# First sums of an MoE loaded after the fourth scatter, sixteen buffers for the late sums, landed blocks counted by ACT

## What is computed

```python
t = _to_tokens(x1)
xf = _ln_t(t).reshape(N, 128)
probs = softmax(xf @ Wr, axis=0)     # xf: 12544 x 128
vals, idx = top_k(probs.T, 1024)                     # per expert
h = gelu(einsum('ecd,edf->ecf', xf[idx], W1) + b1)   # 128 -> 512
out_e = einsum('ecf,efd->ecd', h, W2) + b2           # 512 -> 128
moe = zeros_like(xf).at[idx].add(vals[..., None] * out_e)
x = from_tokens(t + moe)
```

## Time and profile before

| | us |
|---|---|
| time, median of 3 runs | 484.05 (483.96 to 487.23) |
| span of the profiled execution, first to last instruction | 481.8 |
| last gather of expert 7 landed, in that span | 415.4 |
| the fold's last add | 446.9 |
| the last add of the late stage | 478.7 |
| mean granted clock of PE | 0.838 |

### The profile page before, as it was taken

One profiled execution on the slowest core, in us unless ns is written; L12 is line 12 of the kernel. 1 busy time (PEld: TensorE's weight loads), 2 busy tenths in 40 slices (PEclk: granted clock), 3 DMA queues, 4 the chain that ended last, 5 costly groups with the idle time before them and its releaser, 6 DMA issues.

```text
span 481.8 us, 7878 instructions
## 1 busy us (share of the span) xinstructions
PE 356.9 (74%) x2459; PEld 244.9 (51%) x2459; DVE 314.5 (65%) x1047; ACT 256.3 (53%) x526; POOL 158.5 (33%) x151
## 2 busy tenths in 40 slices
PE   2878998999999978201226769797797797498675
PEld 2435655566555647200113557484673765266564
DVE  3278898799899886788796685657552212229544
ACT  3359898789998873676502446254364344320000
POOL 4000000000000000000047777787888787766000
PEclk9989999899999995555555999898989799789655
DMA  4446577766676653992012232443535199737798
GB/s 108 120 122 185 180 227 250 232 195 223 207 244 228 190 171 106 297 353 87 0 28 55 53 96 54 94 47 84 79 44 87 52 236 316 144 29 163 243 374 323
DMA packets 39121, 76.19 MB, mean 158 GB/s; under 512 B 7056, under 2 KB 19504, under 8 KB 39088
## 3 DMA queue, kind: packets, MB, share of 16 engines
q1 hardware_dynamic: 26976, 60.56, 39.7%
q0 software_dynamic: 9472, 8.72, 11.8%
q10 hardware_dynamic: 2640, 6.51, 3.5%
HBM read 35.03 MB, written 30.39 MB: 136 GB/s over the span
## 4 chain that ended last, share of the span: by engine, by line
PE 37%; ACT 18%; DVE 18%; issue 10%; DMA 8%; POOL 6%; SPq 2%; DVEq 0%; ACTq 0%; POOLq 0%
PE psC L898 8%; PE psC L735 6%; ACT ln_tok L547 5%; PE psB L886 4%; DMA x_pad<-moe_sum_late 4%; PE psB L765 4%; PE psC L886 4%; DVE x_all L1426 3%; POOL moe_sum_late L467 2%; PE psB L753 2%; ACT x_in L607 2%; DVE conv L1054 2%; ACT act L570 2%; ACT signs L607 2%; ACT act L586 2%
## 5 line engine op out<-in xcount | busy, mean ns | idle before, releaser
L438 POOL DMA_INDIRECT picked<-token_rows,slot_idx x32 | 31.4, 981 | 249.2 <-issue 248.9
L735 PE MATMUL psC<-x_pad,tap_diag 64*64 64x392 f32 x384 | 72.8, 528 | 8.0 <-issue 4.3
L735 PE MATMUL psC<-hid,tap_turned 64*64 64x392 f32 x384 | 72.8, 528 | 0.0
L898 PE MATMUL psC<-w,hid 128*128 128x128 f32 x448 | 52.9, 280 | 1.8 <-ACT hid L665 1.7
L898 PEld LDWEIGHTS psC<-w,hid 128*128 128x128 f32 x448 | 52.1, 196 | 4.3 <-ACT hid L665 3.4
L735 PEld LDWEIGHTS psC<-x_pad,tap_diag 64*64 64x64 f32 x384 | 29.8, 142 | 39.4 <-issue 32.0
L886 PE MATMUL psB<-picked_T,w 128*128 128x512 f32 x64 | 38.6, 735 | 5.3 <-ACT picked_T L635 5.0
L665 ACT ACTIVATE hid<-psB,b_T 128x512 f32<-128x512 f32 x32 | 21.8, 686 | 37.3 <-PE psB L886 37.3
L547 ACT ACTIVATE ln_tok<-psA,sm 112x128 f32<-112x128 f32 x112 | 40.9, 477 | 0.9 <-DVE sm L1046 0.9
L467 POOL DMA_INDIRECT moe_sum<-y_rows,slot_idx x24 | 37.7, 1572 | 7.3 <-issue 6.4
L1376 DVE TENSOR_TENSOR y_sum<-psC,b_rows 128x512 f32<-128x512 f32 x14 | 9.7, 691 | 44.3 <-PE psC L898 44.3
(11 more groups left out here) (247 smaller groups left out, 802.1 us busy)
## 6 DMA issues: line engine op xcount, KB each, us to landing
token_rows<-rows SPq DMA_DIRECT2D x16, 422.6 KB, 4.9
x_in<-in_x_dram SPq DMA_DIRECT2D x16, 392.0 KB, 3.3
x_res<-in_x_dram SPq DMA_DIRECT2D x16, 392.0 KB, 4.1
moe_sum<-hid SPq DMA_DIRECT2D x16, 392.0 KB, 4.5
x_all<-x SPq DMA_DIRECT2D x16, 392.0 KB, 3.0
moe_sum_late<-hid SPq DMA_DIRECT2D x16, 392.0 KB, 5.1
out_dram<-act ACTq DMA_DIRECT2D x16, 392.0 KB, 5.8
w<-in_L_ffn_W_dram SPq DMA_DIRECT2D x16, 256.0 KB, 3.4
```

The lines of the kernel that those rows point to most:

```text
L438: nc.gpsimd.indirect_dma_start(out=picked_in[k][:, b, :], out_offset=None, in_=rows_dram, in_offset=bass.IndirectOffsetOnAxis(ap=slot_idx[ ...
L735: ins = nc.tensor.matmul(psC[col * HC:col * HC + HC, half, 0:HALF].rearrange("c (h w) -> c h w", w=W), weights[of, n, :], lines[of, q, dy: ...
L898: ins = nc.tensor.matmul((psA if first else psC)[:, h, b * C:(b + 1) * C], hid[:, f, lo:lo + 128], w2[:, q, f * C:(f + 1) * C], start=(f = ...
```

## The change

The sixteen loads of first sums are issued after the weights of expert 6, once scatters 0 to 3 have landed, and ahead of the weights of expert 7; their other waits go. Their buffers no longer include gather buffers or `x_in`: the four convolution buffers become one tensor `work`, of which seven buffers are cut. The fold stays behind the last expert on PE and DVE (`FOLD_SPOTS`: none, none, all sixteen) and has two PSUM regions. The late sums go into the same sixteen buffers, each as soon as its image's first sums are turned and its blocks landed. ACT counts landed blocks after the last gelu, in place of POOL. The output images lie in `hid`. Stores of images 0 to 7 are issued by SP, each behind a late load from the ninth on; ACT issues those of images 8 to 15. In the last expert DVE does bias and weight of the first half ahead of the norm of the second half's rows. Loops over the late images are written out.

```diff
-FOLDED_EARLY = 0
-BEHIND = 2
+FOLD_SPOTS = (range(0, 0), range(0, 0), range(0, B))
+STORED_BY_SP = 8
...
+        work = sb("work", [128, 8 * HW])
+        conv, act1, act2, x1 = (work[:, 2 * HW * n:2 * HW * (n + 1)].rearrange("c (q n) -> c q n", q=2) for n in range(4))
...
+        turned = TPI * C
+        sums_in = [ln_tok[:, 0, :], ln_tok[:, 1, :], x_pad[0:P, 0, 0:turned], x_pad[0:P, 1, 0:turned]] + [
+            work[0:P, n * turned:(n + 1) * turned] for n in range(7)] + [
+            rows[:, 0, 0:turned], rows[:, 1, 0:turned], logits[:, :], logits_T[:, :],
+            s_cmp[0:P, :, :].rearrange("p b k -> p (b k)")]
+        o_img = [hid[:, k:k + 1, 0:HW] for k in range(ENDS)]
         end_regions = (psB, psD, psA, psC)
-        fold_regions = (psD, psA, psB)
+        fold_regions = (psD, psB)
...
-            for e in range(2, E):
+            for e in range(2, E - 1):
                 sp.wait_ge(s_l2, (e - 1) * 2)
                 load_w(e, e % 2)
             for q in range(2):
                 sp.wait_ge(s_sca[q], 16 * SB * SECOND // 2)
-            sp.wait_ge(s_ge, E - 1)
             sp.wait_ge(s_idx, 2 * E)
             for q in range(2):
                 sp.wait_ge(s_rows[q], 16 * B // 2)
                 sp.wait_ge(s_x1c[q], 16 * B // 2)
             for img in range(B):
-                if img == B // 2:
-                    sp.wait_ge(s_l2, 2 * E - 3)
                 load_first(img)
-            sp.wait_ge(s_fd, 2 * ENDS)
+            sp.wait_ge(s_l2, (E - 2) * 2)
+            load_w(E - 1, (E - 1) % 2)
...
-            for img in range(B):
-                if img >= ENDS:
-                    sp.wait_ge(s_ft, img - ENDS + 1)
+            def load_late(img):
+                sp.wait_ge(s_fd, 2 * img + 2)
                 at = LAST_TILES + img
                 sp.wait_ge(s_landed, sp.value_load(need[at:at + 1, 0:1], min_val=1, max_val=SB))
-                load_y(img, img % ENDS)
+                sp.dma_start(sums_in[img].rearrange("p (t c) -> p t c", c=C),
+                             late_t[:, ds(img, 1), :, :].rearrange("p i t c -> p (i t) c")).then_inc(s_yl[img], 16)
+
+            for img in range(B):
+                load_late(img)
+                if img >= B - STORED_BY_SP:
+                    stored = img - (B - STORED_BY_SP)
+                    sp.wait_ge(s_fa, stored + 1)
+                    sp.dma_start(out_d[:, ds(stored, 1), :], o_img[stored % ENDS]).then_inc(s_fo[stored % ENDS], 16)
...
                         nc.gpsimd.indirect_dma_start(out=sums, out_offset=at, in_=y_rows[:, q, b, :],
                                                      in_offset=None, compute_op=ALU.add).then_inc(s_blk[b], 16)
-                        if b >= BEHIND:
-                            pool.wait_ge(s_blk[b - BEHIND], 16)
-                            pool.sem_inc(s_landed, 1)
...
-            for b in range(SB - BEHIND, SB):
-                pool.wait_ge(s_blk[b], 16)
-                pool.sem_inc(s_landed, 1)
...
-            with act.Fori(0, B // ENDS) as turn:
-                for k in range(ENDS):
-                    act.wait_ge(s_fa, turn * ENDS + k + 1)
-                    act.dma_start(out_d[:, ds(turn * ENDS + k, 1), :], o_img[k]).then_inc(s_fo[k], 16)
+            for b in range(SB):
+                act.wait_ge(s_blk[b], 16)
+                act.sem_inc(s_landed, 1)
+            for img in range(STORED_BY_SP, B):
+                act.wait_ge(s_fa, img + 1)
+                act.dma_start(out_d[:, ds(img, 1), :], o_img[img % ENDS]).then_inc(s_fo[img % ENDS], 16)
...
+            def turn_first(img):
+                region = fold_regions[img % 2]
+                pe.wait_ge(s_yf[img], 16)
+                for a, tiles in enumerate(BANK_TILES):
+                    if img >= 2:
+                        pe.wait_ge(s_fk, img * 2 + a - 3)
...
             def last_expert(e, q, use):
                 pe.wait_ge(s_w1[q], use * 16 + 16)
+                pe.wait_ge(s_idx, E * 2)
+                for img in FOLD_SPOTS[0]:
+                    turn_first(img)
                 turn_picked(e, 0)
                 hidden(e, q, 0, {})
                 pe.wait_ge(s_w2[q], use * 16 + 16)
                 down(e, q, 0)
+                for img in FOLD_SPOTS[1]:
+                    turn_first(img)
                 turn_picked(e, 1)
                 hidden(e, q, 1, {})
                 down(e, q, 1)
+                for img in FOLD_SPOTS[2]:
+                    turn_first(img)
...
+            pe.wait_ge(s_fk, 2 * B)
             pe.wait_ge(s_ptc, E * 2)
-            pe.wait_ge(s_yb, 2 * E - 1)
...
-            pe.wait_ge(s_yr, 2 * E)
             pe.wait_ge(s_yb, 2 * E)
...
+            for img in range(B):
+                pe.wait_ge(s_yl[img], 16)
+                if img >= ENDS:
+                    pe.wait_ge(s_fa, img - (ENDS - 1))
                 for t in range(TPI):
+                    ins = nc.tensor.transpose(end_regions[img % ENDS][:, t // 4, (t % 4) * P:(t % 4 + 1) * P],
+                                              sums_in[img][:, t * C:(t + 1) * C], ident[0:P, 0:P])
                 ins.then_inc(s_ft, 1)
...
             def last_expert(e, q, use):
+                for q_of in range(2):
+                    dve.wait_ge(s_x1c[q_of], 16 * B // 2)
...
                         .then_inc(s_gt, 1)
+                    bias_out(e, h)
+                    weigh(e, q, use, h)
                     if h == 0:
                         norm_picked(e, 1)
-                    bias_out(e, h)
-                    weigh(e, q, use, h)
+                    for img in FOLD_SPOTS[1 + h]:
+                        add_first(img)
...
             dve.wait_ge(s_fk, 2 * B)
+            dve.wait_ge(s_l2, 2 * E)
...
+            for img in range(B):
+                k = img % ENDS
                 dve.wait_ge(s_ft, img + 1)
+                if img >= ENDS:
+                    dve.wait_ge(s_fo[k], img // ENDS * 16)
```

More of the change, by code:

```diff
@@ L166, in build @@
         dist = sb("dist", [128, HW])
-        junk = conv[:, :, :].rearrange("c q n -> c (q n)").bitcast(mybir.dt.bfloat16).rearrange("c (k n) -> c k n", n=HW)
+        junk = work[:, 0:2 * HW].bitcast(mybir.dt.bfloat16).rearrange("c (k n) -> c k n", n=HW)
         exps = sb("exps", [128, HW])
@@ L275, in build @@
         s_ge, s_gt = sem("gate_exp"), sem("gate_ready")
-        s_yl, s_fo = ([sem(f"{name}{k}") for k in range(ENDS)] for name in ("y_loaded", "out_stored"))
+        s_yl = [sem(f"late_y_loaded{k}") for k in range(B)]
+        s_fo = [sem(f"out_stored{k}") for k in range(ENDS)]
         s_ft, s_fa = sem("final_turned"), sem("final_added")
@@ L933, in expert @@
                 down(e, q, 1)
+            def turn_first(img):
[4 more added lines that the diff above has]
+                        pe.wait_ge(s_fk, img * 2 + a - 3)
+                    for t in tiles:
+                        ins = nc.tensor.transpose(region[:, a, (t % 4) * P:(t % 4 + 1) * P],
+                                                  sums_in[img][:, t * C:(t + 1) * C], ident[0:P, 0:P])
+                    ins.then_inc(s_fd, 1)
             def last_expert(e, q, use):
                 pe.wait_ge(s_w1[q], use * 16 + 16)
+                pe.wait_ge(s_idx, E * 2)
+                for img in FOLD_SPOTS[0]:
+                    turn_first(img)
                 turn_picked(e, 0)
@@ L956, in _ @@
             first_expert()
             for e in range(1, E - 1):
-                if e == E - 2 and FOLDED_EARLY:
-                    pe.wait_ge(s_idx, E * 2)
-                    pe.wait_ge(s_ptc, (E - 1) * 2)
-                    for img in range(FOLDED_EARLY):
-                        turn_first(img)
-                    pe.wait_ge(s_fk, 2 * FOLDED_EARLY)
                 expert(e, e % 2, e // 2, e + 3 < E, e + 2 < E)
             last_expert(E - 1, (E - 1) % 2, (E - 1) // 2)
-            pe.wait_ge(s_idx, E * 2)
+            pe.wait_ge(s_fk, 2 * B)
@@ L967, in _ @@
             pe.wait_ge(s_ptc, E * 2)
-            pe.wait_ge(s_yb, 2 * E - 1)
-            for img in range(FOLDED_EARLY, B):
-                turn_first(img)
-            pe.wait_ge(s_fk, 2 * B)
             pe.wait_ge(s_gelu, E * 2 * FT)
-            pe.wait_ge(s_idx, E * 2)
-            pe.wait_ge(s_yr, 2 * E)
             pe.wait_ge(s_yb, 2 * E)
-            def turn_back(img, k, turn):
-                pe.wait_ge(s_yl[k], turn * 16 + 16)
-                if since(img, ENDS):
+            for img in range(B):
+                pe.wait_ge(s_yl[img], 16)
+                if img >= ENDS:
@@ L986, in turn_back @@
                 ins.then_inc(s_ft, 1)
-            for k in range(ENDS):
-                turn_back(k, k, 0)
-            with pe.Fori(1, B // ENDS) as turn:
-                for k in range(ENDS):
-                    turn_back(turn * ENDS + k, k, turn)
         @block.vector
@@ L1425, in add_first @@
                     kept = x1_all[:, img * HW + lo:img * HW + lo + n]
```

(16 more changed lines are left out.)

44 lines of the change are left out of this document (2 added, 42 removed).

## The result

The changed kernel takes 479.39 us (median of 4 runs, 478.04 to 480.24) where the kernel before, run beside it, takes 484.38: a ratio of 0.989, 95% interval 0.986 to 0.993. So it is faster, by about the 1% that can be told here. The profiled execution has a span of 478.4 us and took 480.24.

A forecast was written before the change was run, and what follows sets the result against it. Bounds: gather waits, a DVE-paced fold, then DMA-limited late sums after a hole. Fold's end 448.05 + 2.25 + 25.6 + 0.6 gave a 476.5 us span; keeping its 2.25 distance to the median, 478.7 us, range 472 to 486.

The forecast's parts named there:

- one sign that the prediction named for being wrong: Late stage: the forecast is wrong if DVE waits for stores for most of its idle time.
- Gather 6 in the burst: Expert 6's last gather blocks, under the first loads: delayed 6.2 us, landing at 381.6, PE's chain with them.
- Rival 1: Gather 6: its last two blocks each wait for one load, losing 2.1 us, not 6.2; time 474.7; chance 0.22.
- Rival 3: Gather 6: the burst holds the POOL queue until over, landing near 399; 17 us later, 496; chance 0.14.
- Scatter 5: POOL's chain: waits for scatter 4's delayed landing, starting at 392.2 in place of 389.3.
- Order on DVE and the clock: Last expert: second hidden projection 2.1 us later, 0.95 regained by PE's clock; fold starts and ends 1.15 later.
- The fold: Adds of first sums: two regions instead of three cost nothing; upper end 8 us if the cover were gone.
- ACT's count and nine late loads: Around the fold's end: ACT waits for free, and nine late loads fit ahead of the first store, before four.
- The late stage: After the fold: 23 transfers instead of 28, taking 25.6 us, with 2.25 before and 0.6 after; gain 6.4.
- with 1.5 lost: Late stage: 1.5 us lost beyond 24.1 at full rate, some half of the 2.7 lost before.
- rival 2: Late stage: four output images, held until their stores land, bound it at 31.5 us; time 484.6; chance 0.17.

The follow-up runs named there:

- the repeat: The changed kernel run once more without an edit: 479.18 us, ratio 0.988 to the kernel before.
- the best of all: Changed kernel with first loads one at a time, late loads ahead of stores, all stores by ACT, eight output images: 474.36 us, 0.978 to the kernel before.
- both changes: Changed kernel with all late loads ahead by SP, all stores by ACT and eight output images: 475.84 us, 0.989 to the kernel before.

## Why the prediction was right

The forecast was 478.7 us and the result 479.39; it holds, and in part by luck. From gather 6's last block to the end it reckoned with a gain of 5.3 us, a fold 1.15 later and a late stage 6.4 shorter. The profiles show a fold that ends where it did and a late stage 3.7 shorter by the mean of four profiles; more than 1 us of the 5.0 by which the times differ is in neither phase. So two terms were off, in opposite directions, and one sign that the prediction named for being wrong was seen: in the late stage DVE stood idle for 13.5 us (profile after), and 12.5 of them were waits for stores.

- **Gather 6 in the burst.** Predicted 8.8 us from issue to landing, measured 7.71. Expert 7's first down projection was to end 6.2 later; from gather 6 it ends at 44.1 (43.6 in the repeat) instead of 38.1, so 6.0 and 5.5. Of the 6.0, 5.15 are the gather; 0.8 are expert 5's down projection behind the wait, 9.45 us where it took 8.64. Rival 1 would have had 2.56 + 2.1 = 4.7: too little. As that rival uses it, the rule of the Trainium skill ("DMA: Bandwidth & Descriptors", "Queues, rings and completion order") that the engines take turns by packets does not give the size: beside sixteen queued loads the gather's last block lost 5.15 us, beside one load at a time 0.06 (2.62 to landing), and the block that fared worst there 1.3 (3.91).
- **Rival 3** is refuted: gather 6 landed at 378.4, the last load of the burst at 398.3.
- **Scatter 5** started 18.1 us behind gather 6's last block, where 19.4 was predicted (16.5 before), and not for scatter 4's landing: it waited for DVE's rows (the releaser in its row). That sub-step was wrong, and it lay on nothing that ends last.
- **Order on DVE and the clock.** The second hidden projection was to start 2.1 later; from gather 6 it starts at 48.0 and 47.5, against 46.4 and 48.4 before: 0.4 later in the means. The fold was to end 1.15 later; the means are 74.5 and 74.5, nothing. The repeat of the kernel before shows that its own place varies by 0.8, so a term of 1.15 can be neither shown nor refuted by these pairs.
- **The fold** with two regions lasts 15.14 us, as it did (15.13): the cover held, with PE's clock at 1.00.
- **ACT's count and nine late loads** before the fold's end: as predicted, and the first store 2.14 behind it (2.25 predicted). That ACT waits for free holds as long as SP issues the first stores; in the best of all it held one back by 3.4 us.
- **The late stage** was to be 28.45 us from the fold's end, and is 32.1 in the mean of four profiles, where before it was 35.8 in the mean of two. So the gain was 3.7 instead of 6.4. The mis-sized term is "with 1.5 lost": 23 transfers at 1.05 are 24.1 us, and the stage lost some 5 us instead, for two reasons. The loads of images 9 to 15 stand behind stores that wait for adds, so the hole stayed half open (0.68). And SP, with a register read, a load and a store to do for each image, issues its stores up to 2.8 us after their adds, while each of four buffers waits for its store, and DVE with it: rival 2's mechanism, the register read included, but weaker than it would have had it (31.5 of transfers and the same 2.85 around them, 34.4). Leaving SP's eight stores to ACT alone gives 29.2; every kernel in which ACT issues all stores and the fold is in its old place has 27.7 to 29.2, every one in which SP issues eight has 30.7 to 33.3.

What stays open: the late phase with the change's late stage varies between 30.7 and 33.3 from profile to profile, so the parts of the missing 2.7 can't be told apart more finely than that; and the size of what ACT's stores gain rests on phases of one profile each, since the times' intervals overlap. How the gain of the late stage divides between the sixteen buffers and ACT's count of landed blocks was not tried.

## What to carry to other kernels

A burst of loads moved earlier doesn't lose its cost: it moves it to whichever transfer the chain needs next, a gather or a load of weights. Look for what is in flight at the new place, and pace the loads (one in flight) rather than only shifting them. Give stores that free a buffer to an engine that has nothing else to do between them, since in a busy engine's program they wait their turn; four buffers more don't help while that turn sets the pace. And ask whether bytes or waits set the end before adding up gains.

## What the hardware showed unexpectedly

- Full DMA engines don't mean one rate. While late loads and the scatter of expert 7 are under way together, the share is 1.11 to 1.12 at 268 to 274 GB/s (after, 435 to 445). The scatter is not needed for the low rate: with both changes, from 445 to 450, POOL is idle, the last block has landed by 446.6, and mostly late loads run, at 1.05 and 288 GB/s. With loads and stores mixed it is 1.03 at 414 (best, 455 to 460), with stores alone 1.03 at 400 (both changes, 465 to 470). Why the loads by themselves run slower was not tried.
- Which engine issues a store mattered though the DMA engines were nearly full: 29.2 (one profile) against 32.1 us (mean of four). The Trainium skill, "DMA: Bandwidth & Descriptors", "Issuing engines are not separate DMA queues", says that DMAs of several issuers interleave on the same engines and that only issue time is saved. The runs agree: the first eight stores took 5.9 us to landing in the mean from SP and 6.0 from ACT, and what was saved is time in SP's instruction stream, up to 2.8 us a store.
- The stretch ahead of the search's first count took between 194.3 and 199.7 us in the ten profiles of the changed kernel and its variants, whose code there is the same: as much as the whole gain of this change.
